# Holding a software queue's gathers to three blocks ahead of TensorE, and storing the router's pick data with each residual row

## What is computed

```python
x = layernorm(x + mixer(x))                 # 32 heads, causal convolution and decayed scan, 256 -> 2048 -> 256
e = clip(ids, 0, 12499) // 3125             # one of 4 context matrices by token id
x = layernorm(x + (silu(x @ ctx[e].T) * (x @ ctx[e].T)) @ ctx[e].T)
logits = x @ gate_w.T                       # 16 experts, the 2 largest of logits + bias picked
y = sum over the 2 picks of weight * swiglu(x, expert)      # hidden size 176
x = layernorm(x + y + swiglu(x, shared expert))
```

## Time and profile before

| | |
|---|---|
| runs, us | 705.06, 706.42, 706.36, median 706.36 |
| profiled execution, us | 705.55, of which the span is 703.8 |
| busy, us (share of the span) | PE 643.4 (91%), DVE 531.2 (75%), POOL 474.9 (67%), ACT 448.5 (64%) |
| chain that ended last | PE 66%, DVE 13%, issue 6%, ACT 5%, POOL 4%, DMA 2%, another core or an unknown queue 2% |

### The profile page before, as it was taken

One profiled execution on the slowest core, in us unless ns is written; L12 is line 12 of the kernel. 1 busy time (PEld: TensorE's weight loads), 2 busy tenths in 40 slices (PEclk: granted clock), 3 DMA queues, 4 the chain that ended last, 5 costly groups with the idle time before them and its releaser, 6 DMA issues.

```text
span 703.8 us, 11898 instructions
## 1 busy us (share of the span) xinstructions
PE 643.4 (91%) x3514; PEld 492.0 (70%) x3514; DVE 531.2 (75%) x843; ACT 448.5 (64%) x722; POOL 474.9 (67%) x452
## 2 busy tenths in 40 slices
PE   8699999999999999999999999999987997799920
PEld 5477888888878878878888788778856765355510
DVE  4979999999999999999999999769514575122236
ACT  3657788787887887887887878865223554133321
POOL 4276779879878887898798796778242838643044
PEclk9999999999999999999999999999999999789975
DMA  3232112112121131131131121320536912487124
GB/s 152 79 108 92 61 46 102 59 49 65 52 93 60 45 105 60 45 105 60 45 105 60 45 68 36 121 97 15 137 100 157 358 38 84 114 237 188 48 79 130
DMA packets 26999, 65.07 MB, mean 92 GB/s; under 512 B 5571, under 2 KB 18371, under 8 KB 24235
## 3 DMA queue, kind: packets, MB, share of 16 engines
q1 hardware_dynamic: 24139, 56.96, 24.7%
q0 software_dynamic: 2832, 7.75, 4.4%
HBM read 56.42 MB, written 8.28 MB: 92 GB/s over the span
## 4 chain that ended last, share of the span: by engine, by line
PE 66%; DVE 13%; issue 6%; ACT 5%; POOL 4%; DMA 2%; another core or an unknown queue 2%; SPq 0%; POOLq 0%; ACTq 0%; DVEq 0%
PE ps L789 27%; DVE conv L1568 8%; PE ps L817 7%; PE ps L803 5%; PE ps L1067 4%; PE ps L732 3%; PE ps L750 3%; ACT decay L1253 3%; PE ps L1111 3%; DVE decay L1552 2%; PE ps L804 2%; PE ps L772 2%; POOL conv L672 2%; PE ps L826 1%
## 5 line engine op out<-in xcount | busy, mean ns | idle before, releaser
L1568 DVE SCALAR_TENSOR_TENSOR conv<-ps,w_raw,conv 128x506 f32<-128x506 f32 (+3 forms) x352 | 320.3, 933 | 16.1 <-ACT conv L1247 11.4
L789 PE MATMUL ps<-x_hi,w_hi 128*128 128x512 f32 x384 | 158.9, 414 | 7.1 <-DVE conv L1568 6.2
L789 PE MATMUL ps<-x_hi,w_lo 128*128 128x512 f32 x384 | 151.7, 395 | 1.0 <-DVE w_lo L1499 1.0
L1247 ACT ACTIVATE conv<-ps,w_raw 128x512 f32<-128x512 f32 x160 | 108.1, 686 | 68.7 <-PE ps L789 68.5
L789 PE MATMUL ps<-x_lo,w_hi 128*128 128x512 f32 x384 | 150.6, 392 | 0.0
L477 POOL TENSOR_TENSOR decay<-cum_b,cum_tok 128x512 f32<-128x512 f32 (+1 forms) x128 | 103.5, 831 | 15.0 <-DVE cum_tok L1513 15.0
L789 PEld LDWEIGHTS ps<-x_hi,w_hi 128*128 128x128 f32 x384 | 72.5, 189 | 25.9 <-DVE conv L1568 8.2
L483 POOL TENSOR_TENSOR decay<-decay,mask 128x512 f32<-128x512 f32 x64 | 82.4, 1288 | 5.0
L789 PEld LDWEIGHTS ps<-x_hi,w_lo 128*128 128x128 f32 x384 | 72.3, 188 | 18.1 <-DVE w_lo L1499 1.4
L789 PEld LDWEIGHTS ps<-x_lo,w_hi 128*128 128x128 f32 x384 | 72.7, 189 | 12.7
L803 PE MATMUL ps<-conv 128*128 128x256 f32 x256 | 79.5, 392 | 1.8 <-DVE decay L1552 0.3
(11 more groups left out here) (259 smaller groups left out, 1100.5 us busy)
## 6 DMA issues: line engine op xcount, KB each, us to landing
cum_b<-cum_scratch SPq DMA_DIRECT2D x16, 1024.0 KB, 4.7
w_raw<-in_winT SPq DMA_DIRECT2D x16, 778.0 KB, 4.4
y_all<-in_wgu SPq DMA_DIRECT2D x4, 1408.0 KB, 19.4
ys_scratch<-y_blk SPq DMA_DIRECT2D x48, 64.0 KB
late<-in_wdn SPq DMA_DIRECT2D x2, 1408.0 KB
x_scratch<-conv SPq DMA_DIRECT2D x19, 128.0 KB, 3.7
late<-in_woutT SPq DMA_DIRECT2D x1, 2048.0 KB, 9.6
res_scratch<-conv SPq DMA_DIRECT2D x11, 128.0 KB
```

Source lines behind the costliest of these rows:

```text
L789: mm = pe.matmul(ps[:, j % 4, :], wp[:, par, w], xp[:, kk, t], start=(i == 0), stop=(i == 5))
L1247: act.activation(conv[:, par, tile, hf * 512:(hf + 1) * 512], ps[:, j % 4, :], ACT.Copy, scale=w_raw[:, par, tap:tap + 1]).then_inc(S["a_c ...
L1568: dve.scalar_tensor_tensor(out=o[:, :, s:], in0=u[:, :, 0:T - s], scalar=w_raw[:, par, c:c + 1], in1=o[:, :, s:], op0=ALU.mult, op1=ALU.ad ...
```

## The change

`AHEAD = 3`. In the context stage, POOL's gather of block j waits from j = 3 on until PE has turned block j-3. In the expert stage the same rule takes the place of the wait on the ring of eight. The first three expert gathers keep their places between POOL's other work; `add_residual` of the last two blocks now comes ahead of the fourth gather. `meta` moves out of its own tile into four columns behind each row of `xg` (`xg_meta`), and SP stores row and pick data together: 11 stores of rows of 260 numbers in place of 11 stores of rows of 256 and one store of 1408 pieces of 4 numbers. All 11 stores now wait for `v_meta`.

```diff
+AHEAD = 3
...
-        xg = carve(TBS * D).rearrange("p (j d) -> p j d", j=TBS)
+        xg_meta = carve(TBS * RES).rearrange("p (j r) -> p j r", j=TBS)
+        xg, meta = xg_meta[:, :, 0:D], xg_meta[:, :, D:RES]
...
-        meta = take(TBS * 4).rearrange("p (b c) -> p b c", b=TBS)
...
+            sp.wait_ge(S["v_meta"], 2)
             for j in range(TBS):
                 sp.wait_ge(S["p_res"], j + 1)
-                sp.dma_start(res_dram[j * P:(j + 1) * P, 0:D], xg[:, j, :]).then_inc(S["st_res"], 16)
-            sp.wait_ge(S["v_meta"], 2)
-            sp.dma_start(res_dram[:, D:RES].rearrange("(j p) c -> p j c", p=P), meta[:, :, :]).then_inc(S["st_res"], 16)
+                sp.dma_start(res_dram[j * P:(j + 1) * P, :], xg_meta[:, j, :]).then_inc(S["st_res"], 16)
...
-                    sp.wait_ge(S["st_res"], 16 * (TBS + 1))
+                    sp.wait_ge(S["st_res"], 16 * TBS)
...
             for j in range(TBS):
+                if j >= AHEAD:
+                    pool.wait_ge(S["xt1"], j - AHEAD + 1)
                 pool.indirect_dma_start(xg[:, j, :], None, x1_dram,
...
-                if j >= NX:
-                    pool.wait_ge(S["tx_done"], j - NX + 1)
+                if j >= AHEAD:
+                    pool.wait_ge(S["tx_done"], j - AHEAD + 1)
                 pool.indirect_dma_start(xb[:, j % NX, :], None, x2_dram,
...
-                    pool.wait_ge(S["st_res"], 16 * (TBS + 1))
+                    pool.wait_ge(S["st_res"], 16 * TBS)
...
-            for j in range(NX):
+            for j in range(AHEAD):
                 gather_block(j)
                 if j == 0:
                     gate_shared(TBS - 1)
-                elif j <= 4:
+                else:
                     add_residual(TBS - 5 + j)
-            for j in range(NX, NBLK):
+            add_residual(TBS - 2)
+            add_residual(TBS - 1)
+            for j in range(AHEAD, NBLK):
                 gather_block(j)
```

## The result

The changed kernel takes 695.6 us (median of four, 692.9 to 696.8) beside 705.8 (705.1 to 706.4) for the kernel before: ratio 0.984, interval 0.981 to 0.987. In a later set of runs it was 695.1 beside 706.4, ratio 0.983 (0.982 to 0.985). Forecast were 691.6 and a range of 687.5 to 700. So it is faster, by 10 to 11 us where 14 were forecast. The two stalls are gone as forecast; about 6 us come back in two places that the forecast priced at 0 and at 1.

The account below looks back on a forecast made before the run. Late word of finished work beside full-pace POOL gathers was taken to bound the kernel. 705.55 - 5.7 - 10.0 + 0.5 + 0.5 = 690.9, as a median 691.6 us; range 687.5 to 700.

Parts of the forecast that it names:

- What bounds the kernel: Context and expert stages: word of finished work comes late during long runs of POOL gathers at full pace, 1.25 us apart.
- Rival 2: Both stalls: late word has another cause, expert-number reading or small stores, so nothing changes; 704 to 708 us, chance 0.06.
- Context stage, -5.7: Wait on `xt1`: blocks run undisturbed at 2.17 us from block 4, block 10 at 542.1 instead of 547.79; -5.7 us.
- "What shifts with it": 0, at the far end +1: Shared stage: later weight loads and normed-row stores delay POOL's first addition, hidden by DVE's routing; 0, at most +1 us.
- Start of the expert stage, 0.5 + 0.5: Expert stage's first blocks: late gather 2 beside the store burst, and gather 3 behind three additions; 0.5 us each.
- The first 0.5: Expert start: eleven residual stores in a row crowd the gathers, making gather 2 late by 0 to 1.2, value 0.5 us.
- The second: Expert start: three residual additions ahead of gather 3 send it 1.5 later; cost 0 to 0.9, value 0.5 us.
- Expert stage, -10.0: Wait on `tx_done`: blocks run at 2.79 us from block 4, block 20 at 646.9 instead of 656.99; -10.0 us.
- Rival 1: Both gathering stages: only part of the stall goes, or the context stage alone is cured; 697 to 701 us, chance 0.12.
- Rival 3: Both gathering stages: slower, as throttled gathers arrive late and PE waits; 707 to 712 us or more, chance 0.07.
- those of being right: Unnamed pieces gone, context gathers ending near 537, turns at 2.17 and 2.79, block 20 near 642, early expert clock full.
- one sign of being wrong: Shared stage: POOL's first residual addition late by more than 4 us, and its next chain piece late with it.

Follow-up runs that it names:

- ctx_only: Kernel before with only the context stage's gathers held to a lead of three, expert stage and stores unchanged: 701.2 us, ratio 0.994.
- expert_only: Kernel before with only the expert stage's gathers held to a lead of three, in the new order, pick data stored as before: 699.0 us, ratio 0.991.
- meta_only: Kernel before with pick data put behind the residual rows and stored with them, all gathers as before: 706.0 us, ratio 1.001.
- spaced: Kernel before with two POOL memsets ahead of each context gather from the fourth on, no wait for PE: 705.9 us, ratio 1.000.
- pool_direct: Kernel before with plain copies in place of the eleven context gathers, rows unsorted, for timing only: 689.4 us in one run; kernel before 691.2 in that set.
- early_loads: Changed kernel with SP's weight loads started after five context gathers have landed instead of all eleven: 706.1 us, ratio 1.022 against the kernel before.
- loads_split: old_stores with the last two of four big weight loads issued behind the stores of normed rows: 691.7 us, ratio 1.002 against the kernel before.
- after_again: Changed kernel unaltered, run again in a later set beside the kernel before: 695.1 us, ratio 0.983.
- before_again: Kernel before unaltered, run again in a later set: 705.6 us, ratio 0.999.
- lead5: old_stores with a lead of five in place of three, additions left between the gathers: 691.0 us, ratio 1.000 against the kernel before.
- old_stores: Changed kernel with residual rows and pick data stored as in the kernel before, both throttles kept: 693.0 us, ratio 1.001 against the kernel before.
- interleaved: old_stores with one big weight load ahead of every third store of normed rows, not all ahead: 694.0 us, ratio 1.003 against the kernel before.

## Why the prediction was right, and where its terms were off

*What bounds the kernel.* Right for the conditions in which the profile was taken: word of PE's work comes late during long runs of gathers at full pace. ctx_only and expert_only cure one stage each; meta_only cures none; spaced cures the context stage by pacing alone, without a wait, though with a shorter lead as well. How the gathers hold the word back no run shows. The sum of the single gains, 4.5 and 6.7, is 11.3, the gain of the whole 10.2. Rival 2, another cause, is out for these sets: the small stores are in expert_only, and the reading of the expert number is in all.

*The limit of it.* In two of four sets the kernel before has, as far as its time and the expert stage of pool_direct tell, no stall to lose, and there no throttled kernel gained anything (1.000, 1.001, 1.002, 1.003). Five of its 38 runs there took 696.3 to 699.3, above all the others (688.2 to 695.1); whether these had one of the stalls, no trace shows. What decides between the two cases stays open. It is not the kernel, nor one chip that always does it: sets one and four, 705.7 and 690.3, bear the same chip number. There is no trace of the kernel before itself from a set at 691, and the changed kernel was not run in one. By its own losses (2.9 in the shared stage, up to 3.5 in the start) it would be some us slower there than the kernel before, and this is an estimate from these rows, not a measurement.

*Context stage, -5.7.* Measured 5.8. The lead of three is enough, as argued: with the loads kept behind, every gather from the third on came in time; early_loads shows what a gather of 12.5 us does to it.

*"What shifts with it": 0, at the far end +1.* Measured +2.9; this term was mis-sized, for three reasons. The forecast took the near edge of its own estimate, 569.4 to 570.4, for the end of loads and stores. With the start 0.6 later that is 570.0; POOL's first addition began at 571.30, 1.3 later: SP's own queue stood still for 6.5 us at 558.15 behind 7 MB of loads, and the last store took 4.90 more to land. Then the three additions and two gatings took 4.65 and not 3.5 (0.90 for two of the additions, 1.57 for one gating). With 0.2 to spare in the forecast, L655 comes at 575.95 and not at 573.7, 2.3 late. The last 0.6 is PE's half clock behind that wait, which the forecast did not count. Stores ahead of the last loads take this back: loads_split, with two fifths of the loads behind the stores, has POOL's 1.93 of cover by DVE again.

*Start of the expert stage, 0.5 + 0.5.* Measured 3.5, and 1.7 in after_again, or only 0.3 there against before_again in the same set. The first 0.5, the lateness of gather 2, was 1.0, inside its range of 0 to 1.2. The second, for the order of POOL's work, was 0: gather 3 went 1.4 later behind gather 2 than before, and PE did not wait for it. What is missing in the sum is a term for the clock: 2.5 us at the 1.2 GHz level after PE's wait of 1.7. The forecast counted a wait as its own length. Why gather 2 landed later, by the burst or by chance, is not shown: it took 5.4, 5.0 and 5.6 to its use with the burst and the new order (after, after_again, early_loads), but also 5.0 in before_again, with nothing changed, against 4.4 in before.

*Expert stage, -10.0.* Measured 10.0, block 4 to block 20.

*Rival 1* (part of the stall stays) is out: no piece without a name is left. That the time of the profiled execution nearly reached its 697 comes from the two terms above. *Rival 3* is real as a mechanism (early_loads) and doesn't occur in the change. The rule of the Trainium skill cited against the change (DMA: Bandwidth & Descriptors, "Rules for kernel authors": issue early, wait late) fails where words come late, by the 10 us of this change, and in a set without the stall a lead of eight was neither better nor worse than one of five (lead5, 1.000).

*Signs and sums.* Of the signs that the prediction named, those of being right came true in the context stage and from block 4 on. Two did not: the clock was at half and not at full in the early expert stage, and block 20 was turned at 648.1 and not near 642. And one sign of being wrong did come: POOL's first addition waited 5.91, with L655 late behind it. The terms of the forecast's own range add up to 690.6 to 695.9, where it says 690 to 695; the stated 687.5 to 700 holds either. Two terms were off by 5.4 together, and the profiled run was 5.9 above the forecast for it, 690.9; the median was only 4.0 above, because the profiled run was the slowest of four. That the distance is no larger on the median is luck of the draw.

## What to carry to other kernels

Before a pause that no row names is cured, the kernel before should be timed in several sets on several chips: a cure is worth only as much as the disturbance is there, and here it was there in the first runs and in two later sets of four. When the last of a row of transfers is delayed, everything that a queue holds behind it moves as well, first the loads and then the small stores that someone does wait for; price the landing of the last of them, not the end of the loads. Put stores that an engine waits for ahead of the last large loads. And a wait of TensorE for a transfer can cost more than its length: look at the granted clock behind it, and count that too.

## What the runs showed of the hardware

- The same kernel took 705.7 and 706.4 us in two sets and 690.3 and 691.2 in two others, each median over 13 to 20 runs. In traces of the slower sets there are two pauses in which the word of finished work is late, with idle times of 3.2 to 6.4 us; what makes a set slow or quick was not found.
- A gather of 128 rows took 0.95 on POOL with 0.30 between two of them, and 3.5 to 5.6 from issue to use where TensorE waited for it; beside 7 MB of loads one took 12.5 (early_loads).
- SP's queue stood for 6.50 to 6.51 us on one store behind four large loads, in after, ctx_only, spaced and old_stores alike.
- A wait of TensorE of 1.7 us (busy 0.28 of 2) was followed by 6 us at the 1.2 GHz level in after; waits of 1.3 to 2.1 us were followed by some 3 us at it in after_again, before_again, pool_direct, early_loads, interleaved and old_stores. Waits of 1.1 in loads_split and 1.4 in expert_only were followed by none. At that level two blocks of the expert stage took 7.7 us in place of 5.2.
